# Two attention stages of a fused kernel: the bias made on the array with keys on the partitions, and the first scores moved ahead of half of the projections

## The reference

```python
def _tri_att(z, lnw, lnb, qw, kw, vw, bw, gw, gb, ow, ob):
    x = _ln(z, lnw, lnb)
    bias = jnp.einsum('bijc,ch->bhij', x, bw)[:, None]
    q = (x @ qw)... / sqrt(CA);  k = (x @ kw)...;  v = (x @ vw)...
    a = jnp.einsum('bihqc,bihkc->bihqk', q, k) + bias
    p = jax.nn.softmax(a, axis=-1)
    o = jnp.einsum('bihqk,bihkc->bihqc', p, v)...
    o = o * jax.nn.sigmoid(x @ gw + gb)
    return o @ ow + ob
```

## Time and profile before

| | |
|---|---|
| median of 3 runs | 263.08 us (261.41 to 264.0) |
| the profiled execution | 262.68 us |
| its span (first to last instruction) | 260.9 us |
| TensorE busy in the span | 233.7 us (90%) |
| DVE, ACT, POOL busy | 145.1, 127.4, 105.4 us |
| mean granted TensorE clock | 0.961 |
| attention `ta0`, `ta1` | from 74.7 to 134.8 us, from 142.8 to 199.8 us |

### The profile page before, as it was taken

The page is one execution under the profiler, slowest core; times in us unless marked ns, Lnnn a source line. Parts: engine busy times, 40 slices in busy tenths (PEclk is TensorE's granted clock), DMA queues, the critical chain, the costliest instruction groups (busy, mean ns, idle before and its releaser), DMA issues.

```text
span 260.9 us, 6408 instructions
## 1 busy us (share of the span) xinstructions
PE 233.7 (90%) x2722; PEld 126.9 (49%) x2722; DVE 145.1 (56%) x238; ACT 127.4 (49%) x225; POOL 105.4 (40%) x108
## 2 busy tenths in 40 slices
PE   7987999999999879999679987899967997899993
PEld 4665543775344435655334343565643524465541
DVE  0443546437774766576213274675742346999970
ACT  2865387475483657566337546675665631000001
POOL 5000002040211338867910003788795000689891
PEclk9999599889999999999858999999999999999999
DMA  6419000404042000000000100000000000000002
GB/s 215 168 17 325 12 0 34 133 20 143 1 144 47 3 0 3 5 0 4 6 0 0 30 3 0 3 4 3 3 3 3 1 0 19 0 0 0 0 3 80
DMA packets 5820, 9.34 MB, mean 36 GB/s; under 512 B 1952, under 2 KB 4064, under 8 KB 5632
## 3 DMA queue, kind: packets, MB, share of 16 engines
q1 hardware_dynamic: 5312, 8.76, 10.3%
q10 hardware_dynamic: 288, 0.16, 0.2%
q0 software_dynamic: 192, 0.00, 0.0%
HBM read 6.59 MB, written 2.23 MB: 34 GB/s over the span
## 4 chain that ended last, share of the span: by engine, by line
PE 58%; POOL 17%; issue 8%; ACT 7%; DVE 6%; DMA 1%; POOLq 1%; ACTq 0%; DVEq 0%
POOL lnroom L424 10%; PE psum L829 7%; PE psum L840 6%; PE psum L985 5%; PE psum L1015 4%; PE psum L1065 3%; PE psum L904 3%; POOL soft L396 3%; PE psum L1009 3%; PE psum L821 3%; POOL og L410 3%; PE psum L885 3%; PE psum L1106 3%; PE psum L1085 3%; PE psum L1052 2%
## 5 line engine op out<-in xcount | busy, mean ns | idle before, releaser
L396 POOL TENSOR_TENSOR soft<-soft,rinv 128x512 f32<-128x512 f32 x32 | 33.4, 1042 | 19.2 <-DVE rinv L754 18.4
L741 DVE TENSOR_REDUCE mx<-psum 128x8 fp32r<-128x512 f32 x32 | 21.4, 673 | 19.0 <-PE psum L1015 19.0
L554 ACT ACTIVATE soft<-psum 128x512 f32<-128x512 f32 x32 | 19.1, 597 | 18.8 <-PE psum L1065 18.8
L1065 PE MATMUL psum<-cst,soft 128*128 128x128 f32 x128 | 21.3, 290 | 3.0 <-POOL soft L396 1.2
L1152 PE MATMUL psum<-lnroom,cst 128*128 128x512 f32 x48 | 22.8, 598 | 1.2 <-POOL lnroom L424 1.2
L751 DVE TENSOR_REDUCE rsum<-soft 128x8 f32<-128x512 f32 x32 | 21.6, 674 | 3.5 <-ACT soft L548 3.5
L410 POOL TENSOR_TENSOR og<-gth,y 128x256 f32<-128x256 f32 x30 | 21.7, 729 | 3.1 <-ACT y L560 3.1
L387 POOL TENSOR_SCALAR gth<-gth 128x512 f32<-128x512 f32 x16 | 9.5, 618 | 32.5 <-ACT gth L541 32.5
L548 ACT ACTIVATE soft<-psum 128x512 f32<-128x512 f32 x32 | 19.1, 597 | 5.0 <-PE psum L1070 5.0
L1065 PEld LDWEIGHTS psum<-cst,soft 128*128 128x128 f32 x128 | 13.7, 142 | 13.7 <-ACT soft L554 7.8
L589 ACT ACTIVATE Y<-psum 128x512 f32<-128x512 f32 x2 | 1.1, 594 | 38.7 <-PE psum L1152 38.7
(11 more groups left out here) (144 smaller groups left out, 438.3 us busy)
## 6 DMA issues: line engine op xcount, KB each, us to landing
gth<-inv_w SPq DMA_DIRECT2D x1, 1600.0 KB, 8.4
hop<-vals SPq DMA_DIRECT2D x2, 512.0 KB, 2.7
vals<-hop SPq DMA_DIRECT2D x8, 128.0 KB, 3.0
tmw<-tm_w SPq DMA_DIRECT2D x2, 384.0 KB, 4.3
z0R<-z_rows SPq DMA_DIRECT2D x2, 256.0 KB, 3.7
z0T<-z_cols SPq DMA_DIRECT2D x1, 512.0 KB, 5.7
hop<-gate SPq DMA_DIRECT2D x1, 512.0 KB, 2.6
z1T<-hop SPq DMA_DIRECT2D x4, 128.0 KB, 3.0
```

The costliest lines, as they stand in the source:

```text
L396: pool.tensor_tensor(PN[u % 2][:, :].rearrange("p (a k) -> p a k", k=N), E_[u % NE][:, :].rearrange("p (a k) -> p a k", k=N), rinv[:, 8 * ...
L741: nc.vector.tensor_reduce(mx[:, 8 * t:8 * t + 8], bank[t % 4].rearrange("p (a k) -> p a k", k=N), AX_X, ALU.max, negate=True).then_inc(sig ...
L1065: last = nc.tensor.transpose(bank[T_BANK][:, 128 * h:128 * h + 128], PN[u % 2][:, 128 * h:128 * h + 128], K("ident"))
```

## The change

The DRAM round of the bias is gone. For the bias product `x` is now the stationary operand: 32 products for each attention, 16 for each half, with a stationary 32 x 128 block of `x` and only 4 moving columns (the heads), written to banks 2 to 5, one bank for each of the four channel blocks. So the result has keys on the partitions. ACT and DVE copy it, two copies each, into `braw`, and `bst` then has keys on its partitions where it had queries.

With this layout `bst` is the stationary operand of the bias product of the scores, and `pairr` is streamed. The stationary operand holds at most 128 columns, so the one 128 x 512 product for each tile becomes four of 128 x 128, one for each head.

The order of the first part of each attention is another. The factors are made in two halves. The first four tiles of scores stand before the second half of the factors, and eight tiles stand before the second half of the gates; the second halves of values and gates come later, and the loop over `t` starts at 3.

```diff
-        YBANKS = ((2, 3, 6, 7), (0, 1, 4, 5))
-        VBANKS = ((2, 3, 6, 7), (0, 1, 4, 5))
-        GBANKS = ((2, 3, 6, 7), (4, 5, 6, 7))
+        YBANKS = ((0, 1, 6, 7), (4, 5, 6, 7))
+        VBANKS = ((2, 3, 4, 5), (4, 5, 6, 7))
+        GBANKS = ((4, 5, 6, 7), (4, 5, 6, 7))
+        BIAS_BANK = 2
...
-                sp.wait_ge(sig(f"{st}_brow"), at(f"{st}_brow", 2))
-                sp.dma_start(bias_hop[s][:, :], brow).then_inc(sig(f"{st}_bias_hop"), 16)
-                sp.wait_ge(sig(f"{st}_bias_hop"), at(f"{st}_bias_hop", 16))
-                for part in range(2):
-                    sp.dma_start(braw[part * N:(part + 1) * N, :].rearrange("q (h k) -> q h k", h=H),
-                                 bias_hop[s].rearrange("(h g) (r k) -> (g r) h k", h=H, k=N)).then_inc(sig(f"{st}_braw"), 16)
...
+                act.wait_ge(sig(f"{st}_bproj"), at(f"{st}_bproj", 2))
+                for dup in range(2):
+                    nc.scalar.activation(bias_rows(dup, 0), bias_part(0), ACT.Copy).then_inc(sig(f"{st}_b_act"), 1)
...
+                factors_out(0)
+                values_from(0)
                 for g in range(GB):
                     gate(0, g)
-                for t in range(TILES + LAG_A):
-                    if LAG_T <= t < TILES + LAG_T:
+                exponentials(0)
+                exponentials(1)
+                factors_out(1)
+                exponentials(2)
+                exponentials(3)
+                values_from(1)
+                for g in range(GB):
+                    gate(1, g)
+                for t in range(LAG_T, TILES + LAG_A):
+                    if t < TILES + LAG_T:
                         transposed_out(t - LAG_T)
...
+                dve.wait_ge(sig(f"{st}_bproj"), at(f"{st}_bproj", 2))
+                for dup in range(2):
+                    nc.vector.tensor_copy(bias_rows(dup, 1), bias_part(1)).then_inc(sig(f"{st}_b_dve"), 1)
...
+                pe.wait_ge(sig(f"{st}_ln_logv"), at(f"{st}_ln_logv", 2))
                 for ch in range(2):
                     pe.wait_ge(sig(f"{st}_ln_x"), at(f"{st}_ln_x", ch + 1))
-                    mm(bank[4 + ch][0:16, :], taw[:, w0 + 256:w0 + 272], half(x, ch), start=True, stop=True).then_inc(sig(f"{st}_bproj"), 1)
+                    for j in range(4 * ch, 4 * ch + 4):
+                        for g in range(GB):
+                            last = mm(bank[BIAS_BANK + g][:, H * j:H * j + H], x[C * g:C * g + C, 2 * j * N:(2 * j + 2) * N],
+                                      taw[C * g:C * g + C, w0 + 256 + g:w0 + 272 + g - GB + 1:GB], start=True, stop=True, skip_group_check=True)
+                    last.then_inc(sig(f"{st}_bproj"), 1)
...
                     for t in (2 * p, 2 * p + 1):
-                        mm(bank[t % 4], pairr[:, :], bst[:, :], start=True, stop=False, skip_group_check=True)
+                        for h in range(H):
+                            mm(bank[t % 4][:, 128 * h:128 * h + 128], bst[:, 128 * h:128 * h + 128], pairr[:, :], start=h == 0, stop=False,
+                               skip_group_check=True)
...
+                factors(0)
+                pe.wait_ge(sig(f"{st}_b_act"), at(f"{st}_b_act", 2))
+                pe.wait_ge(sig(f"{st}_b_dve"), at(f"{st}_b_dve", 2))
                 values(0)
-                values(1)
+                pe.wait_ge(sig(f"{st}_bst"), at(f"{st}_bst", 2))
...
+                scores(0)
                 pe.wait_ge(sig(f"{st}_v_act"), at(f"{st}_v_act", 2))
                 pe.wait_ge(sig(f"{st}_v_dve"), at(f"{st}_v_dve", 2))
                 gates(0)
...
                 scores(1)
+                lower(0)
+                lower(1)
+                pe.wait_ge(sig(f"{st}_g_act"), at(f"{st}_g_act", 4))
+                factors(1)
+                lower(2)
+                lower(3)
+                pe.wait_ge(sig(f"{st}_exp"), at(f"{st}_exp", 2))
+                scores(2)
...
+                values(1)
+                pe.wait_ge(sig(f"{st}_exp"), at(f"{st}_exp", 4))
+                scores(3)
                 pe.wait_ge(sig(f"{st}_v_act"), at(f"{st}_v_act", 4))
                 pe.wait_ge(sig(f"{st}_v_dve"), at(f"{st}_v_dve", 4))
                 gates(1)
```

114 lines of the change are left out of this document (58 added, 56 removed).

## The result

| | before | after |
|---|---|---|
| median of 4 runs, same chip | 263.54 us (261.41 to 266.77) | 275.36 us (274.2 to 277.67) |
| ratio, 95% interval | | 1.050 (1.043 to 1.057) |
| profiled execution: time, span | 262.68, 260.9 us | 276.0, 274.2 us |
| mean granted clock in it | 0.961 | 0.931 |

The change makes the kernel 5.0% slower, 11.8 us. That is inside the stated range (265 to 283) and outside the likeliest case's own (265 to 273); the forecast was 5.9 us, half of it. The kernel has no single time, since from run to run TensorE spends more or less of it at the lower of its two clock levels, and medians of four runs carry some of that.

The account below looks back on a forecast made before the run. TensorE, busy 90% of the span, was taken as the bound. Scores 5.9 us, making the bias 0.2, waits and rounding -0.2 gave 5.9 us more: 268.6 profiled, median about 269.0 us, 2.3% slower, range 265 to 283.

Parts of the forecast that it names:

- the likeliest case: Whole kernel: about 269.0 us, 265 to 273 with its clock cases; chance 0.62.
- the bias product: Scores: eight narrow products at 0.109 us make a call 1.04 us instead of 0.67; 16 calls cost 5.9 us.
- the sum: Whole kernel: 5.9 us for scores, 0.2 for making the bias, -0.2 for waits and rounding, 5.9 us slower.
- Rival (a): Scores' bias product: narrow float32r products run slower than wide ones, 0.22 us each, giving 282 us; chance 0.25.
- rival (b): Scores' bias product: loads are hidden, 0.055 us each, no slowdown, 263.5 us; chance 0.09 together with the order winning.
- the order: First part of each attention: new waits of 3.4 us replace old ones; worth 0, plus or minus 1 us.
- The four waits: First part: 0.46 us before second gates, 0.78 before first transposes, 1.8 before second transposes, 0.38 once for POOL.
- the walk: Both kernels followed through their waits using row lengths: +3.0 us for the first attention, +2.9 for the second.
- the making and the DRAM round: Before the scores: removing the round gives 0; making the bias moves the end by at most 0.1 to 0.2 us per attention.
- The cover: After the making: `bst` ready at some 79.0 us, first scores need it at 81.5, so 2.5 us and nothing to pay.
- rival (c): Attention ends: the low-clock stretch costs about 3.7 us; escaping it gives 265.3; left as is, both cases in the range.
- at both ends: Clock case: the changed kernel falls into low clock at the end of both attentions, 272.7 us.

Follow-up runs that it names:

- experiment 2: Kernel before with only the scores' bias product cut into four 128 x 128 products (biases wrong, for time alone): 275.9 us, kernel before beside it 265.0.
- experiment 9: Kernel before, old order, bias made on the array without DRAM, turned back by four transposes, wide bias product in scores: 270.1 us, ratio 1.013 (0.990 to 1.035).
- experiment 1: Changed kernel with the scores' bias product as one 128 x 512 product again (biases wrong, for time alone): 272.6 us, kernel before beside it 265.0.
- experiment 13: Changed kernel plus small unused products (128 x 128 in waits, one 128 x 256 last) at the end of each attention: 268.15 us, ratio 1.011 (0.997 to 1.025).
- experiment 12: Kernel before plus small unused products (128 x 128 in waits, one 128 x 256 last) at the end of each attention: 261.72 us, ratio 0.990 (0.985 to 0.996).
- experiment 5: Changed kernel with the array-made bias turned back by four transposes, and the wide 128 x 512 bias product in the scores: 273.5 us, kernel before beside it 263.0.
- experiment 8: Changed kernel with bias turned back by transposes, wide bias product, and unused 128 x 256 products at both attentions' ends: 267.6 us, ratio 1.014 (1.008 to 1.020).
- experiment 4: Kernel before with only the new order of the first part, keeping DRAM round and wide bias product: 283.7 us, ratio 1.076 (1.066 to 1.086).
- experiment 10: Kernel before in its old order with array-made bias, no DRAM round, and narrow bias products in the scores: 277.4 us, ratio 1.050.

## Why the prediction was right in its sign and half the size

**Right: the bias product.** 1.04 us a call and a period of 4.65 us, both as worked out from the transposes' row and the narrow float32 row. Alone in the kernel before it costs 6.6 us without low time (experiment 2) against 5.9 in the sum. The traces say it more sharply. Five kernels have full clock in `ta1` from the first factor to the second out-projection, all eight calls of `scores` between them (windows; the kernel before; experiment 9, the making alone; experiment 1, making and order; experiment 2, the narrow product alone; experiment 13, all three):

```profile
144.81:187.87 43.06, 39.59 (x628) 22.14 (x627) 26.25 (x52) 25.46 (x51) 22.55 (x28) 1.00 0.03 7
146.87:189.91 43.04, 40.12 (x634) 22.32 (x630) 27.09 (x54) 25.47 (x52) 22.55 (x28) 1.00 0.01 2
148.81:192.37 43.56, 39.71 (x630) 22.09 (x626) 27.13 (x54) 25.76 (x51) 22.50 (x28) 1.00 0.01 2
154.11:200.09 45.98, 42.51 (x675) 27.43 (x675) 26.25 (x52) 25.46 (x51) 22.57 (x28) 1.00 0.03 6
147.08:192.89 45.81, 42.50 (x678) 27.45 (x674) 27.14 (x54) 25.88 (x52) 22.48 (x28) 1.00 0.01 2
```

The narrow product alone is 45.98 - 43.06 = 2.92 us for eight calls, where the sum had 8 x 0.37 = 2.96. Rival (a), a slow pace for narrow float32r, would have shown 0.22 us a product, and rival (b) 0.055; neither is there. The figure of the Trainium skill (TensorE: Matmul & The Clock Gate, "Back-to-back issue gap"), 81 ns a pair, is too cheap for these pairs: the call has 1.04 us and not 0.85.

**Right: the order is worth nothing by its waits.** The four waits came where the walk had them, within 0.25 us each, and the whole change in these windows is 45.81 - 43.06 = 2.75 us, where the walk had 2.9. One thing the sum did not say: the terms don't add. With the wide product the new order costs 43.56 - 43.04 = 0.5 us for each attention, and with the narrow one nothing; the narrow product costs 2.92 us in the old order and 45.81 - 43.56 = 2.25 in the new one, where part of it runs inside waits that the order has anyway. The column without low time has the same signs with larger numbers for both attentions (2.5 us for the order, experiment 1 against 9, and 6.6 against 3.7 for the narrow product); the windows put them at 1.0, 5.8 and 4.5. The walk gave only the whole, and that was right. A slip in rival (b), which changes no chance: its 263.5 adds 0.4 us that the 263.1 already holds.

**Right: the making and the DRAM round.** +0.9 us without low time for both attentions (experiment 9, the turning included), 0.2 us for the making in `ta0` and nothing in `ta1` in the ledger, and nothing in the windows above (43.04 against 43.06). The cover was there: `bst` was ready at 80.2 us, and the first scores began at 84.5.

**Wrong: rival (c), "I leave it as it is".** This is the step that failed. The prediction took the clock for a thing of one place, the end of an attention, with 3.7 us to win or lose. It left it as it was, and so put the change's own clock term at 0; the first factors, at full clock before, had no such term at all. What the runs showed in its place is a term of 4 to 6 us. In the profiled executions it is 7.5 us, of which 3.5 stand in the first factors, 3.0 at the two ends (+3.9 and -0.9) and 1.0 in code that the change left alone; the case "at both ends", which the prediction had at 272.7, came true there, and the factors came on top. Over all runs the mean low time rises from 26 to 38 us, and 12 us at 0.30 are 3.7 us, a low price, since this pair paid 7.5 us for 17 us of added low time. Taken from the other side, the change costs 5.8 us in stretches at full clock and 11.8 in all, which leaves 6.0; by the column without low time it costs 7.1 (264.1 - 257.0), which leaves 4.7. With smaller fillers at the ends, so that both kernels have 16 or 17 us of low time, 6.4 us are left of the 11.8 (experiments 12 and 13). So the mechanism of the forecast's sum was right, and the missing term is the clock's. The prediction named the sign itself: it would be wrong "if the low clock comes at other places". That came.

**What the extra low time comes from, as far as it is shown.** First the making, in `ta0`. The first factors were low in all ten profiled kernels that make the bias on the array, and in none of the six that don't. Neither 4 or 64 moving columns, nor 32 or 128 rows, nor the order of what follows, nor one filler product behind each half changed that. But the fall is not always behind the making: it began between 0.5 us after the making's start (experiment 13) and 3.3 us after it (the changed kernel, 1 us into the factors), and in five of the ten inside the making. On the timeline of PE of experiment 13, where the clock went low at 74.2 us:

```profile
71.66 2.05 PE L891 MATMUL psum<-soft 32*128 32x128 f32 x16
73.71 3.18 PE L1012 MATMUL psum<-taw,x 32*128 32x4 f32 x64
```

The 16 narrow records of L891 stand straight ahead of the making in `ta0` only. In `ta1` ten filler records of 128 x 256 stand there (2.32 us), and the first factors were low in three profiles of ten (the changed kernel, experiments 5 and 8). That the two stretches of narrow products matter together is a rival that no experiment tested; fillers between them would tell.

Second the ends. The end of `ta0` was low in all ten profiles without fillers, the kernel before among them; the end of `ta1` in those of the changed kernel and of experiments 2 and 4; and in the six profiles with fillers neither end was. The fillers took 21 us of low time from the changed kernel (38 to 17) and 10 from the kernel before (26 to 16), so with the ends filled the extra low time is 1 us in place of 12. Most of it therefore goes with the ends, although the factors of `ta0` stay low with fillers too.

Third, none of this is a matter of one part of the change. The narrow product alone (experiment 2) and the making alone (experiment 9) have a mean low time of 39 us each, both together in the old order 53 (experiment 10), and all three parts 38. Why the clock falls at the making stays open: no experiment removed the fall there while leaving the making in. Each kernel has one profile, and some of the falls are chance; that the mean low time differs (38 against 26 us) rests on 4 and 27 runs.

**For this kernel:** the change isn't worth having in any of the forms tried; the kernel before with small fillers is.

## What to carry to other kernels

Cost a wide product that is cut into narrow ones by its loads, and a new order by a walk through its waits: both came out here to a few tenths of a microsecond. Then look at the clock line of the profile, and where it shows a place that falls, ask of each new stretch of short products or waits whether the clock can fall in it, and price that with the rows at either level; a kernel that runs near full clock can lose as much there as by its added work. When two kernels are compared, put each run's granted clock beside its time: here 0.30 us per us of low time explains most of a spread of 8 us. Such a correction tells 2 us and not 1; a stretch that has full clock in both traces tells tenths.

## What the runs showed of the hardware

- A float32r load and product pair of 128 x 128 goes at 0.11 us, the pace of the load (eight loads from 108.06 us on take 0.97 us, the last of them 0.19), the same as for float32 (0.111); float32r does not load faster (191 ns a load in the trace, 188 for the wide form, 190 for the float32 factors of the kernel before).
- A us at 1.2 GHz costs 0.30 us of time on average in this kernel, but 0.5 in the first factors, where TensorE never waits (5.33 us at a mean of 0.68 against 3.57).
- The granted clock can fall in or just behind a stretch in which TensorE is as good as never idle: in `ta0` in ten profiles of ten, where 2.05 us of narrow products and 2.2 us of the making stand in a row, and in three of ten in `ta1`, where 2.3 us of 128 x 256 products stand ahead of the making.
- It falls at the end of `ta0` in ten profiles of ten without fillers, where TensorE waits 0.6 to 0.7 us between its products.
- Products of 128 x 128 whose result nobody reads, put in waits of 0.7 us, keep the clock up there: low time from 26 to 16 us, and 1.0% less time in the kernel before (ratio 0.990).
